# Label bias and mask of the graph attention: three GpSimd operations in place of two VectorE operations

## The reference

```python
self_feat = vcq @ W_self.T + b_self
for d in range(2):
    A = adj_f if d == 0 else jnp.swapaxes(adj_f, 1, 2)
    A = A[:, :, :NONGT, :]             # 20 neighbours, 11 labels
    cond = A.sum(-1)
    vb = A @ w_bias + b_bias
    # in _gat_attention: qh, kh with 16 heads
    aff = jnp.einsum('bnhd,bmhd->bnhm', qh, kh) * (1.0 / np.sqrt(dh))
    mask = cond_adj[:, :, None, :] > 0
    aff = jnp.where(mask, aff, NEG) + label_bias[:, :, None, :]
    w = jax.nn.softmax(aff, axis=-1)
    ...
```

## Time and profile before

| What | Value |
|---|---|
| Median of 3 runs | 2933.77 us (2932.55 to 2938.58) |
| The profiled execution's own time | 2933.84 us |
| Its span in the profile | 2932.0 us |
| PE busy | 2852.8 us (97% of the span) |
| PEld busy | 2443.1 us (83%) |
| DVE busy | 2217.6 us (76%) |
| ACT busy | 1603.7 us (55%) |
| POOL busy | 1041.9 us (36%) |
| Mean granted TensorE clock | 0.991 of full speed |

### The profile page before, as it was taken

One profiled execution on the slowest core, in us unless ns is written; L12 is line 12 of the kernel. 1 busy time (PEld: TensorE's weight loads), 2 busy tenths in 40 slices (PEclk: granted clock), 3 DMA queues, 4 the chain that ended last, 5 costly groups with the idle time before them and its releaser, 6 DMA issues.

```text
span 2932.0 us, 68187 instructions
## 1 busy us (share of the span) xinstructions
PE 2852.8 (97%) x27746; PEld 2443.1 (83%) x27746; DVE 2217.6 (76%) x2956; ACT 1603.7 (55%) x3252; POOL 1041.9 (36%) x675
## 2 busy tenths in 40 slices
PE   8899999999999999999999999999999999979998
PEld 6888889999887777777777777777788999979998
DVE  4689986555546888888888888888577766677876
ACT  2566653332214777777777777777233556544442
POOL 1122110000001444444444444447466555563332
PEclk9999999999999999999999999999999999989999
DMA  7132236653695433333333333332664554577775
GB/s 238 53 118 78 89 123 219 221 216 101 218 317 147 117 88 88 88 94 89 88 94 89 89 94 88 94 98 72 204 226 166 205 205 192 225 242 237 242 244 173
DMA packets 277104, 445.06 MB, mean 152 GB/s; under 512 B 37848, under 2 KB 152696, under 8 KB 273224
## 3 DMA queue, kind: packets, MB, share of 16 engines
q1 hardware_dynamic: 267940, 434.48, 45.9%
q0 software_dynamic: 576, 6.29, 0.5%
q10 hardware_dynamic: 8292, 0.05, 0.2%
HBM read 266.99 MB, written 173.74 MB: 150 GB/s over the span
## 4 chain that ended last, share of the span: by engine, by line
PE 62%; DMA 2%; POOL 2%; DVE 1%; ACT 1%; SPq 1%; issue 0%; POOLq 0%; ACTq 0%; DVEq 0%
PE b_po L1850 16%; PE b_ps L1821 13%; PE b_tp_act L1833 8%; PE d_pm L2515 8%; PE d_pm L2527 4%; PE c_po L2102 4%; PE d_spare L2527 3%; PE d_pt L2527 3%; PE b_tp_dve L1833 2%; PE d_spare L2515 1%; DMA c_ot<-o_t 1%; POOL w_raw L113 1%; POOL d_blocks L2374 1%; PE d_pt L2506 0%; DMA d_x_second_raw<-hidden_blocks 0%
## 5 line engine op out<-in xcount | busy, mean ns | idle before, releaser
L1878 DVE TENSOR_REDUCE head_nm<-b_ps 128x1 f32<-128x1024 f32 x510 | 599.5, 1217 | 16.4 <-PE b_ps L1821 3.3
L1789 ACT ACTIVATE b_p<-b_ps,head_nm 128x1024 f32<-128x1024 f32 x510 | 562.6, 1113 | 0.0
L1850 PE MATMUL b_po<-b_pt,b_v 128*64 128x256 f32 x4096 | 498.4, 385 | 0.8 <-DVE b_pt L1898 0.8
L1794 ACT ACTIVATE b_pt<-b_tp_act 128x512 f32<-128x512 f32 x512 | 308.2, 602 | 306.9 <-PE b_tp_dve L1833 306.9
L1898 DVE COPY b_pt<-b_tp_dve 128x512 f32<-128x512 f32 x512 | 351.4, 687 | 116.6 <-PE b_tp_dve L1833 116.6
L1833 PEld LDWEIGHTS b_tp_act<-ident,b_p 64*128 64x128 f32 x4096 | 311.2, 138 | 122.0 <-issue 100.4
L1850 PEld LDWEIGHTS b_po<-b_pt,b_v 128*64 128x64 f32 x4096 | 272.1, 136 | 128.4 <-ACT b_pt L1794 0.9
L1833 PE MATMUL b_tp_act<-ident,b_p 64*128 64x64 f32 x4096 | 347.4, 225 | 2.4 <-issue 2.4
L1833 PE MATMUL b_tp_dve<-ident,b_p 64*128 64x64 f32 x4096 | 347.9, 225 | 0.0
L1833 PEld LDWEIGHTS b_tp_dve<-ident,b_p 64*128 64x128 f32 x4096 | 311.6, 138 | 10.7
L2374 POOL TENSOR_TENSOR d_blocks<-d_blocks 128x512 f32<-128x512 f32 x128 | 189.7, 1482 | 111.8 <-ACT d_blocks L2426 104.9
(11 more groups left out here) (442 smaller groups left out, 7616.6 us busy)
## 6 DMA issues: line engine op xcount, KB each, us to landing
b_raw_q<-q_t SPq DMA_DIRECT2D x124, 256.0 KB, 4.3
x_mlp_raw<-hidden_blocks SPq DMA_DIRECT2D x112, 256.0 KB, 3.7
d_x_second_raw<-hidden_blocks SPq DMA_DIRECT2D x112, 256.0 KB, 3.2
hidden_blocks<-d_blocks SPq DMA_DIRECT2D x32, 768.0 KB, 3.3
k_t<-p_out SPq DMA_DIRECT2D x64, 256.0 KB, 2.2
q_t<-p_out SPq DMA_DIRECT2D x64, 256.0 KB, 2.3
v_n<-p_out SPq DMA_DIRECT2D x64, 256.0 KB, 3.5
b_v<-v_n SPq DMA_DIRECT2D x32, 512.0 KB, 3.9
```

Of the source, the lines that this page charges most:

```text
L1789: act.activation(pr[k % 4][:], ps[k % 2][:], ACT.Exp, bias=nm[:, k % 4:k % 4 + 1], accum_out=rs[:, n:n + 1]).then_inc(exp_done, 1)
L1794: act.activation(dst, src, ACT.Copy).then_inc(t_out[0], 1)
L1850: mm = pe.matmul(po[rows, (blk % 2) * 2 * P:(blk % 2 + 1) * 2 * P], vt[u][:, kc, rows], pt[blk % 2][h][:, kc, :], start=(kc == 0), stop=(k ...
L1878: dve.tensor_reduce(nm[:, k % 4:k % 4 + 1], ps[k % 2][:], axis=AX.X, op=ALU.max, negate=True).then_inc(max_done, 1)
```

## The change

The part of `bias` behind the two reductions moves from VectorE to GpSimd. VectorE keeps the two reductions; each now raises a new semaphore, `adj_sums`, and VectorE waits for it before it gives `prod` and `adj` free. GpSimd gets a function `bias(k)` with three operations on 40 columns: the compare and multiply into row 2 (behind the first reduction), the addition of b_bias to row 0 in place (behind the second), and, behind a wait for both of its own results, the sum into row 3. Each raises `bias_done`. GpSimd calls `bias(k + 1)` at the head of its turn k, ahead of the subtraction of `SPLIT` and of the wait for relu of tile k. VectorE's `softmax(k)` waits for `bias_done` before it adds the bias (not for k = 0, whose bias `graph_tables` still makes on VectorE).

Two semaphores are saved: `id_ready` is merged into `pool_done` (so each wait on it counts 2 more, and TensorE waits for 2 of `pool_done`), and `half_set` into `zeros_set`. The diff, without the hunks that only rename or renumber these:

```diff
...
@@ -379,10 +379,10 @@
 
         @block.gpsimd
         def _(pool):
-            pool.memset(ident[:], 0.0).then_inc(id_ready, 1)
-            pool.wait_ge(id_ready, 1)
+            pool.memset(ident[:], 0.0).then_inc(pool_done, 1)
+            pool.wait_ge(pool_done, 1)
             pool.affine_select(out=ident[:], in_=ident[:], compare_op=ALU.not_equal, fill=1.0, base=0,
-                               pattern=[[-1, P]], channel_multiplier=1).then_inc(id_ready, 1)
+                               pattern=[[-1, P]], channel_multiplier=1).then_inc(pool_done, 1)
             pool.memset(silu_t[:], 0.0).then_inc(pool_done, 1)
             pool.memset(bq8[:], 0.0).then_inc(pool_done, 1)
             pool.memset(q8[:], 0.0).then_inc(pool_done, 1)
...
@@ -781,9 +781,20 @@
             for k in range(2, 4):
                 pool.memset(x5[k][:, F + 1:F + 4:2], 1.0).then_inc(zeros_set, 1)
 
-            pool.memset(half[:], -0.5).then_inc(half_set, 1)
+            pool.memset(half[:], -0.5).then_inc(zeros_set, 1)
             pool.sem_inc(x_free, 4)
+            def bias(k):
+                s = sm[k % 2]
+                pool.wait_ge(adj_sums, 2 * k - 1)
+                pool.tensor_scalar(s[:, 2, :], s[:, 1, :], 0.0, NEG, ALU.is_le, ALU.mult).then_inc(bias_done, 1)
+                pool.wait_ge(adj_sums, 2 * k)
+                pool.tensor_tensor(s[:, 0, :], s[:, 0, :], wrow[:, L0:L0 + 1].to_broadcast([P, HJ]), ALU.add).then_inc(bias_done, 1)
+                pool.wait_ge(bias_done, 3 * k - 1)
+                pool.tensor_tensor(s[:, 3, :], s[:, 0, :], s[:, 2, :], ALU.add).then_inc(bias_done, 1)
+
             for k in range(B * BT):
+                if k + 1 < B * BT:
+                    bias(k + 1)
                 if k in SPLIT:
                     b, c = SPLIT[k]
                     pool.wait_ge(gp_high, KC * (b - 1) + c + 1)
@@ -793,7 +804,7 @@
                 pool.wait_ge(y_done, k + 1)
                 pool.sem_inc(x_free, 1)
                 if k == LN0 + GT:
-                    pool.wait_ge(half_set, 1)
+                    pool.wait_ge(zeros_set, 7)
                     pool.wait_ge(var_ready, 1)
                     pool.tensor_tensor(rstd[:], ve[:], half[:], ALU.pow).then_inc(rstd_ready, 1)
 
@@ -1002,14 +1013,11 @@
 
                 s = sm[k % 2]
                 dve.wait_ge(adj_in[k % 2], 16 * (k // 2 + 1))
-                link(dve.reduce_sum(s[:, 1, :], adj[k % 2][:].rearrange("p l j -> p j l"), axis=AX.X))
-                dve.tensor_scalar(s[:, 2, :], s[:, 1, :], 0.0, NEG, ALU.is_le, ALU.mult)
+                dve.reduce_sum(s[:, 1, :], adj[k % 2][:].rearrange("p l j -> p j l"), axis=AX.X).then_inc(adj_sums, 1)
                 dve.wait_ge(prod_done, k + 1)
-                link(dve.reduce_sum(s[:, 0, :], prod[:].rearrange("p l j -> p j l"), axis=AX.X))
+                dve.reduce_sum(s[:, 0, :], prod[:].rearrange("p l j -> p j l"), axis=AX.X).then_inc(adj_sums, 1)
+                dve.wait_ge(adj_sums, 2 * k)
                 dve.sem_inc(prod_read, 1)
-                i = dve.scalar_tensor_tensor(out=s[:, 3, :], in0=s[:, 0, :], scalar=wrow[:, L0:L0 + 1], in1=s[:, 2, :],
-                                             op0=ALU.add, op1=ALU.add)
-                link(i)
                 dve.sem_inc(adj_used, 1)
 
             def first_rows(k):
@@ -1040,6 +1048,8 @@
                 if k >= 2:
                     dve.wait_ge(wt_done, k - 1)
                 z = lg[k % 2]
+                if k:
+                    dve.wait_ge(bias_done, 3 * k)
 
                 for n in range(2):
                     i = dve.tensor_tensor(
```

More of the change, by code:

```diff
@@ L265, in graph_tables @@
             "act_out dve_out gh_done gl_done")
[L266 to L267 removed]
+        (b_mod_in, silu_done, mod_done, mod_t_done, mod_rows_done, mod_rows_t, gates_done, gates_copied) = sems(
+            chain, nc, "tables", "b_mod_in silu_done mod_done mod_t_done mod_rows_done mod_rows_t gates_done gates_copied")
         ws_in, ws_x_in, ws_n_in, wk_in, wq_in, wo_in, css_out, out_done, gates_out = sems(
@@ L329, in _ @@
             act.dma_start(bk[:], t["bk"].rearrange("d (k p) -> p (d k)", p=P), allow_slow_non_contiguous=True).then_inc(s_in, 16)
-            act.wait_ge(pool_done, 2)
+            act.wait_ge(pool_done, 4)
             act.dma_start(bq8[:, :, B], t["bq"].rearrange("d (k p) -> p (d k)", p=P), allow_slow_non_contiguous=True).then_inc(s_in, 16)
-            act.wait_ge(pool_done, 4)
+            act.wait_ge(pool_done, 6)
             act.dma_start(rowb[B:B + 1, 0, :], t["b_self"].rearrange("(a n) -> a n", a=1)).then_inc(s_in, 16)
@@ L438, in _ @@
             mm.then_inc(q_done, 1)
-            pe.wait_ge(id_ready, 2)
+            pe.wait_ge(pool_done, 2)
             pe.wait_ge(dve_step, 4)
@@ L556, in _ @@
             dve.wait_ge(q_done, 2)
-            dve.wait_ge(pool_done, 3)
+            dve.wait_ge(pool_done, 5)
             dve.tensor_copy(q8[:, :, 0:B], ps[7][:, 0:KC * TW].rearrange("p (k b) -> p k b", b=TW)[:, :, 0:B])
@@ L563, in _ @@
             dve.tensor_copy(wsh[:], ws_t[:, 0:KC, :]).then_inc(ws_done, 1)
-            dve.wait_ge(pool_done, 5)
+            dve.wait_ge(pool_done, 7)
             for dc in range(2 * KC):
@@ L613, in _ @@
                     ALU.add).then_inc(mod_t_done, 1)
-            dve.wait_ge(pool_done, 6)
+            dve.wait_ge(pool_done, 8)
             dve.wait_ge(m1_copied, 2 * KC)
@@ L693, in graph_attention @@
         ws_done, raw = tables_end.ws_done, tables_end.raw
-        gp_high, gp_rest = sems(chain, nc, "graph", "gp_high gp_rest")
+        gp_high, gp_rest, adj_sums, bias_done = sems(chain, nc, "graph", "gp_high gp_rest adj_sums bias_done")
         (zeros_set, dve_step, o_done, a_done, lg_done,
@@ L702, in graph_attention @@
         wqk_in, w2_in, w_scaled, w_sums, w_high, w_rest = sems(chain, nc, "graph", "wqk_in w2_in w_scaled w_sums w_high w_rest")
-        (rows_in, half_set, stats_done, aggr_done, var_ready, rstd_ready, z_done, zt_done, xm_done, xb_sums, xb_high, xb_rest, y1_in) = sems(
-            chain, nc, "graph", "rows_in half_set stats_done aggr_done var_ready rstd_ready z_done zt_done xm_done xb_sums xb_high xb_rest y1_in")
+        (rows_in, stats_done, aggr_done, var_ready, rstd_ready, z_done, zt_done, xm_done, xb_sums, xb_high, xb_rest, y1_in) = sems(
+            chain, nc, "graph", "rows_in stats_done aggr_done var_ready rstd_ready z_done zt_done xm_done xb_sums xb_high xb_rest y1_in")
         y_out = sems(chain, nc, "graph", " ".join("y_out%d" % i for i in range(2)))
```

## The result

| | before | after |
|---|---|---|
| Median of 12 runs | 2935.18 us (2931.28 to 2939.33) | 2941.03 us (2936.51 to 2948.48) |
| Ratio to before | | 1.0019, 95% interval 1.001 to 1.0027 |
| Span of the profiled execution | 2932.0 us | 2946.5 us |
| First and last start of the bias addition | 104.35, 410.76 us | 105.39, 417.59 us |
| Graph stage between these | 306.41 us | 312.20 us |

The kernel became slower by 0.19%, 5.85 us by the medians; 2940.7 us was forecast. The profiled execution of after was the longest of its twelve, so its 14.5 us more of span are not the difference. By place they are 1.04 us ahead of the stage, 5.79 in it, some 1.3 up to the attention (its first b_po matmul comes at 926.7 and 934.8 us), nothing through the attention and 6.4 in the last 870 us, where the code is the same. The medians differ by what the stage differs.

A forecast was written before the change was run, and what follows sets the result against it. TensorE and VectorE were taken to hand the bound to and fro; after the change, a closed loop through GpSimd sets the step. Terms by kinds of step summed to +6.85 us on 2933.84: 2940.7 us, 8-in-10 range 2931 to 2953.

The forecast's parts named there:

- The queue: On GpSimd, bias(k+1) waits behind the x addition `yo` until 8.37 us into the step, though the reductions are there at 7.7.
- The size of the chain: From `yo`'s end to VectorE's bias addition: waits, compare, two additions and signal, 1.18 us, for a step of 9.55 us.
- The seven steps: Steps 9 to 11 and 17 to 20: VectorE's subtraction comes before GpSimd's table subtraction, not behind it; -6.7 us together.
- What goes: VectorE loses L1006 (0.10 us) and L1010 (0.57 us), worth little since its next two-SBUF-input operation waits for `yo` anyway.
- steps 5 to 8: Graph stage steps, 35.0 us before, were to become 38.2 us: +3.2 us.
- The count: Graph stage: a chain shorter by c saves c in some 29 steps.
- steps 1 to 4: Step 1 loses 0.9 us, steps 2 and 3 are swallowed by ScalarE's stall for x behind table loads; +1.8 us.
- A sign that was wrong: In regular steps VectorE was to be idle some 0.7 us before the bias addition, released by GpSimd.
- (a): Rival, faster: GpSimd's three operations nearly free at 0.1 us each, chain 0.73 us, sum -6.2, 2927.6 us; chance 0.10.
- (c): Rival, much slower: each small GpSimd operation costs half a microsecond, chain 1.93 us, sum +28, 2962 us; chance 0.12.
- (b): Rival, no measurable change: chain 0.85 to 1.1 us, sum -2.7 to +4.5, centre 2935 us; chance 0.20.
- (d): Rival: VectorE no less loaded, TensorE's slack covers the longer GpSimd queue; 2928 to 2934 us, centre 2931; chance 0.06.

The follow-up runs named there:

- e3: The changed kernel with GpSimd's last addition done twice, the second behind a wait for the first; median 2952.97 us, ratio 1.006 to before.
- e9: The changed kernel with only the compare ahead of GpSimd's addition of tile k-1 (`yo`); median 2933.33 us, ratio 0.9997 to before.
- e1: The changed kernel with all of GpSimd's bias(k+1) ahead of its addition of tile k-1 (`yo`); median 2947.76 us, ratio 1.0035 to before.
- e4: The kernel before, with GpSimd's table subtraction held until VectorE has subtracted the maximum in the next step; median 2924.8 us, ratio 0.9964.
- e5: The changed kernel with GpSimd's table subtraction held until VectorE has subtracted the maximum in the next step; median 2945.26 us, ratio 1.0035 to before.
- e11: The kernel before with the table subtraction held likewise and only the compare moved to GpSimd, ahead of `yo`; median 2927.68 us, ratio 0.9969.
- e2: The changed kernel without GpSimd's addition of b_bias; median 2936.23 us, ratio 1.0007 to before.

## Why the prediction was right

**The queue.** The bias does stand behind `yo`, and `yo` does stay at 7.07 us. e3 and e9 change the chain behind `yo` and the regular steps follow to the hundredth (+0.35, -0.43). e1 shows that the crossing alone costs no more than VectorE did.

**The size of the chain.** Forecast 1.18 us, measured 1.36. The additions were right (0.25 and 0.27 for 0.26 and 0.28), by the line through 512 and 640 elements. The compare was too small, 0.35 for 0.21: I had taken it below a select over 128 elements (0.289), and why it takes longer is not shown. The first wait took 0.20 for 0.18, the signal took 0.13 for 0.07, and the pause of 0.08 between compare and addition had no term, while the wait between the additions was 0.08 and not 0.18. Hence 9.71 and not 9.55 us.

**The seven steps.** -7.73 for -6.7. The order was forecast (VectorE's operation at `yo`'s end, then GpSimd, then the table); e4 and e5 show that it is this order that pays.

**What goes.** That the removed operations are worth little by themselves is shown by e11 for the compare; for L1010 it is only argued. The argument, that the next operation with two SBUF inputs is held to the end of `yo` anyway, covers only steps in which one follows. In steps 5 to 8 L1045 follows, which has one input in SBUF, and L1010 with its signal stood right ahead of it (0.22 us of waiting at 177.47). What its removal alone would bring there no run shows; the sum does not use it, since the loop through GpSimd sets those steps.

**The count.** Taking c off the chain was to save c in 29 steps. e3 (11.0 us for 0.35, 31 times) agrees; in e2 and e9 step 4 returns about a microsecond, because the table loads set it. In steps 1 to 4 the sum was near (+1.55 for +1.8), but not by its terms: counted from the first bias addition the queue of the table loads did start 1.15 us later, yet its 20 loads took 8.10 us instead of 9.02 (over the kernels here they take anything between), so the stall ended only 0.5 us later.

**A sign that was wrong.** VectorE was to stand idle for some 0.7 us ahead of the bias addition. It is 2.16 us in a regular step and 1.27 on average (38.1 in 30). The prediction's own numbers, reductions done at 7.7 and the next addition at 9.55, leave 1.8; the 0.7 did not enter the sum. L1076 came at 1.62 to 1.65 us for 1.8.

**The error that cancelled.** The chain was 0.18 us too short, which makes steps 5 to 8, 12, 23 and 24 together 1.1 us longer than forecast; the seven steps and steps 16, 25 and 26 came out 1.7 us better, and the rest 0.5. The sum was 1.06 us too high, and the 2933.84 us that it started from lies 1.34 below the median of twelve runs. The mechanism is shown; that the total lies within 0.4 us of the median is partly luck, two errors of opposite sign, as is the side of 0.2% on which 0.19% falls.

**The rivals.** (a) and (c) fall with the durations, 0.25 to 0.35 us an operation, (b) with the chain of 1.36 us, though the total lies close to it. (d) falls with VectorE's 38.1 us of waiting and with e3: TensorE's slack did not cover the loop. It was wrong too that VectorE would be no less loaded (36.40 of 50 us for 44.98).

## What to carry to other kernels

Before moving small work to an idle engine, look at what stands ahead of it in that engine's queue when its input is ready, and count the queue, the waits and the signal, in each turn of the closed loop. Before pushing an operation back, look at what it gives free. And where two engines exclude each other on their operands, first try a wait that puts the long operation beside instructions that don't stand against it: that one line brought 0.36% here (7.7 us in the stage), where moving the work cost 0.19%.

## What was not expected of the hardware

On GpSimd the compare and multiply of 40 elements with one input takes longer (0.35 us at least) than an addition with two inputs (0.25 to 0.27). A VectorE operation that waits for GpSimd gets its turn as soon as GpSimd's operation ends, ahead of the next one in GpSimd's queue if that comes 0.2 us later: in step 11 L1086 ran first and the compare, begun at 221.62, was done only at 222.71. Held so by a long subtraction, the compare takes 1.09 or 1.10 us in steps 13, 14 and 18 to 20 too.
